# Routed expert layer on one core: when second choices are dispatched, which drain closes a stage, and where the second group's gate stands

## The reference, cut to what matters

```
logits = xf @ gate_w + gate_b
top_vals, top_idx = top_k(softmax(logits), 2)            # 16 experts, 2 chosen
a = silu(xf @ w1[e] + b1[e]) * (xf @ w3[e] + b3[e])      # inner width 176
y = sum over the two choices of  top_val * (a @ w2[e] + b2[e])
z = silu(xf @ sw1 + sb1) * (xf @ sw3 + sb3) @ sw2 + sb2  # shared expert, width 352
x = x + 0.5 * (y + z)
```

## Time and profile before

| what | value |
|---|---|
| median of 3 runs | 1052.64 us (1049.37, 1052.64, 1054.99) |
| the profiled execution's own time | 1053.46 us |
| its span in the trace | 1051.7 us |
| granted TensorE clock, mean | 0.891 |
| busy: TensorE / VectorE / ScalarE / POOL | 803.1 / 588.3 / 468.7 / 590.6 us |
| `front` first pass, `experts`, `attention` | about 0 to 238, to 443.8, to 589.5 us |
| `front` second pass, `experts`, `combine` | to 811.0, to 1017.5, to 1051.7 us |
| sends of `front` (L316) | 256, 252.8 us busy |

### The profile page before, as it was taken

The page is one execution under the profiler, slowest core; times in us unless marked ns, Lnnn a source line. Parts: engine busy times, 40 slices in busy tenths (PEclk is TensorE's granted clock), DMA queues, the critical chain, the costliest instruction groups (busy, mean ns, idle before and its releaser), DMA issues. The chain is left out here.

```text
span 1051.7 us, 20394 instructions
## 1 busy us (share of the span) xinstructions
PE 803.1 (76%) x5408; PEld 718.9 (68%) x5409; DVE 588.3 (56%) x1989; ACT 468.7 (45%) x926; POOL 590.6 (56%) x600
## 2 busy tenths in 40 slices
PE   2899999607999999328989489999810999999910
PEld 2677787507999999326777468877710999999910
DVE  6577766404555555256885477776600555555526
ACT  3466564104555555134664256575200555555500
POOL 2446777753777777532220146677774477776730
PEclk9999999858999999757999679998965999999965
DMA  9812221312333333232200001111231333333339
GB/s 276 118 38 60 66 63 51 95 43 77 101 103 101 103 104 96 68 133 81 80 0 1 0 22 34 40 49 49 61 88 39 89 101 101 103 101 103 94 132 374
DMA packets 82819, 90.42 MB, mean 86 GB/s; under 512 B 20414, under 2 KB 69451, under 8 KB 80715
## 3 DMA queue, kind: packets, MB, share of 16 engines
q1 hardware_dynamic: 63052, 45.42, 16.9%
q0 software_dynamic: 17408, 35.95, 10.2%
q10 hardware_dynamic: 2304, 8.39, 2.0%
HBM read 47.46 MB, written 44.37 MB: 87 GB/s over the span
## 5 line engine op out<-in xcount | busy, mean ns | idle before, releaser
L873 POOL DMA_INDIRECT ys<-e_y,e_x x288 | 275.8, 958 | 139.8 <-issue 87.8
L316 POOL DMA_INDIRECT xs<-f_xrow,f_slot x256 | 252.8, 987 | 87.6 <-issue 75.3
L992 PE MATMUL e_py<-w,e_at 97*128 (+1 forms) x1152 | 152.2, 274 | 0.0
L992 PEld LDWEIGHTS e_py<-w,e_at 97*128 97x128 f32 (+1 forms) x1152 | 139.9, 191 | 0.2 <-issue 0.2
L917 ACT ACTIVATE e_xth<-e_px 128x256 fp32r<-128x256 f32 x144 | 55.2, 384 | 171.4 <-PE e_px L956 171.4
L897 DVE TENSOR_TENSOR e_a<-e_pu,e_sil 128x352 f32<-128x352 f32 x144 | 75.5, 525 | 96.9 <-ACT e_sil L923 91.6
L956 PE MATMUL e_px<-ident,e_x 128*128 128x128 f32 x288 | 57.7, 282 | 90.7 <-DMA e_x<-xs 86.4
L904 DVE TENSOR_SCALAR e_y<-e_py,e_x 128x128 f32<-128x128 f32 x288 | 87.8, 346 | 58.0 <-PE e_py L992 57.9
L756 PEld LDWEIGHTS f_pz<-sw,f_gated 128*128 128x128 f32 (+1 forms) x768 | 102.6, 195 | 9.3
L649 ACT ACTIVATE f_sil<-f_phg,sb 128x512 f32<-128x512 f32 (+1 forms) x96 | 64.7, 685 | 97.9 <-PE f_phg L742 97.6
L468 DVE SCALAR_TENSOR_TENSOR f_gated<-f_phg,sb,f_sil 128x512 f32<-128x512 f32 (+1 forms) x96 | 71.7, 747 | 63.8 <-ACT f_sil L649 54.4
(11 more groups left out here) (160 smaller groups left out, 1431.7 us busy)
## 6 DMA issues: line engine op xcount, KB each, us to landing
e_x<-xs SPq DMA_DIRECT2D x288, 65.0 KB
t_yt<-ys SPq DMA_DIRECT2D x8, 1024.0 KB, 4.9
c_yt<-ys SPq DMA_DIRECT2D x8, 1024.0 KB, 10.4
ys<-e_y,e_x POOLq DMA_INDIRECT x288
xa<-in_attn_x ACTq DMA_DIRECT2D x8, 512.0 KB, 10.3
xs<-f_xrow,f_slot POOLq DMA_INDIRECT x256, 2.4
out<-xa ACTq DMA_DIRECT2D x8, 512.0 KB
f_raw<-in_ffn_w SPq DMA_DIRECT2D x32, 88.0 KB
```

What stands on the lines that cost most here:

```text
L316: pool.indirect_dma_start(xs, bass.IndirectOffsetOnAxis(slot[:, q, i:i + 1], 0), xrow[:, i, :], None).then_inc(done, 16)
L873: pool.indirect_dma_start(ys, bass.IndirectOffsetOnAxis(xin[r][:, t, D:D + 1].bitcast(I32), 0), y[r][:, t, :], None).then_inc(sent[r], 16)
L992: last = pe.matmul(p_y[r][:, t * D:(t + 1) * D], at[r][0:rows_, q], w2, start=c == 0, stop=c == 1, skip_group_check=True)
```

## The change

Three things are changed.

1. POOL's loop sends the second choices of group g - 1, no longer of g - 2, behind the first choices of group g, and ends one turn earlier. To that end `rewrite(s - 2)` on VectorE moves from the end of step s to a place ahead of hot(s) in the same step.
2. In step 1 alone, hot(1), sums(1) and places(1) on VectorE stand directly behind indices(1), and count(1) on TensorE stands ahead of the first `ups`.
3. All four kinds of Blocks are opened with `no_gpsimd_drain=True`: at the Block's end the other engines execute a plain DRAIN and then all five meet at a barrier of semaphores alone, without POOL's DRAIN. `phase` is not touched.

```diff
-        with nc.Block() as block:
+        with nc.Block(no_gpsimd_drain=True) as block:
...
-                for g in range(GROUPS + 2):
+                for g in range(GROUPS + 1):
...
-                    if g >= 2:
-                        pool.wait_ge(rewrote, g - 1)
+                    if g >= 1:
+                        pool.wait_ge(rewrote, g)
                         pool.sem_inc(passed, 1)
-                        send(g - 2, 1, sent1)
+                        send(g - 1, 1, sent1)
...
                     if gating:
                         largest(s)
                         indices(s)
+                    if s == 1:
+                        hot(s)
+                        sums(s)
+                        places(s)
                     gates(m)
...
                     gates(m + 2)
-                    if gating:
+                    if s >= 2:
+                        rewrite(s - 2)
+                    if gating and s != 1:
                         hot(s)
...
-                    if gating:
+                    if gating and s != 1:
                         sums(s)
...
-                    if gating:
+                    if gating and s != 1:
                         places(s)
...
-                    if s >= 2:
-                        rewrite(s - 2)
...
                         if i == 0 and gating:
                             gating_mm(s)
+                        if i == 0 and s == 1:
+                            count(s)
                         ups(m)
...
                         if i == 3 and gating:
-                            count(s)
+                            if s != 1:
+                                count(s)
```

## The result

| | before | after |
|---|---|---|
| median of the runs | 1053.82 us (4 runs, 1049.37 to 1055.17) | 1027.74 us (4 runs, 1026.74 to 1029.63) |
| the profiled execution's own time | 1053.46 us | 1027.63 us |
| its span | 1051.7 us | 1025.9 us |
| mean granted TensorE clock | 0.891 | 0.892 |

The ratio is 0.9762 (95% interval 0.9728 to 0.9796): 26 us faster. The forecast was 1045.8 us, and the result lies outside its range; the first rival, "the drains vanish", had 1029.3 us.

The account below looks back on a forecast made before the run. POOL's sends without a pause were taken to bound front. 1053.46 - 16.6 (part 1) + 9.8 (part 2) + 0 (part 3) = 1046.7 us, or 1045.8 us against the runs' median; range 1040 to 1051.5 us.

Parts of the forecast that it names:

- the drains vanish: Rival: the four long POOL DRAINs at the ends of front and experts go away; 16.5 us gained, 1029.3 us, chance 0.13.
- this end of the sum: Part 3's upper end at the Block ends: 16.5 us gained if the DRAIN's length hangs on the first barrier alone.
- cover of some 0.6 us: At stage ends, clearing semaphores ahead of the L72 DRAIN could cover this much per stage if it is partly plain waiting.
- both theories: At stage ends: the L72 DRAIN pays in full (0 us gained), or the long DRAINs vanish (16.5 us gained).
- The SBUF rule: GpSimd cannot write descriptors during VectorE two-port operations: 620 ns alone, 3100 overlapped; 40 us more if all 16 moved sends met one.
- the 1.9 us for the clock: Part 2, step 1 on TensorE: the pause delays the clock's rise, costing 0.4 + 1.5 us in the two passes.
- the 7.9 us of plain delay: Part 2, step 1: first `ups` wait 4.6 us longer per pass; less savings, 4.2 and 3.7 us.
- the 651 us expected for the second run: Second pass: POOL's run of sends without a pause was to begin at the `scales` of group 4, about 651 us.
- The change to the order brings nothing: Rival: step 1's pause or VectorE's mid-step waits cancel part 1; within 3 us of 1052.6, say 1051 us, chance 0.08.
- The clock stays low: Rival: TensorE's granted clock stays at 0.5 through step 1; part 2 costs 27.3 us, total 1063 us, chance 0.05.

Follow-up runs that it names:

- e5: The changed kernel with a plain POOL DRAIN added at the end of front and experts, in the second pass behind four tiles of zeros; 1044.4 us (one run).
- e6: The changed kernel with a full barrier put into `phase` ahead of the clearing of semaphores; 1042.93 us, ratio 0.9925 to the kernel before.
- e7: The changed kernel with plain POOL DRAINs ahead of the last 8 sends, behind the landing (two in a row in the second pass) and at experts' start; 1034.34 us.
- e1: The kernel before with only the Blocks' end changed (`no_gpsimd_drain=True` at all four Blocks); 1035.49 us, ratio 0.9857.
- e3: The changed kernel without the early gate, step 1 as before (parts 1 and 3); 1020.84 us, ratio 0.9704 to the kernel before.
- e4: The changed kernel without the early dispatch, second choices two groups behind as before (parts 2 and 3); 1042.80 us, ratio 0.9919 to the kernel before.
- e2: The changed kernel with the old Block end at all four Blocks (parts 1 and 2); 1043.39 us, ratio 0.9923 to the kernel before.
- e8: The kernel e3 with second choices of groups 0 and 1 sent without lag and their rewrites moved along; 1019.21 us, ratio 0.9709 to the kernel before.
- e9: The kernel e8 with second choices of group g - 1 ahead of `scales(g + 3)` and later rewrites at their step's end; 1009.91 us, ratio 0.9597.

## Why the prediction was wrong, and where it was right

**Part 3 failed, and it is 16.0 of the 18.1 us by which the forecast missed.** The step is the sentence "I take it that the L72 DRAIN becomes that one and pays in full: 0 us". Right was that a DRAIN is long where it is the first plain one behind sends (e5, e6, e7) and that the long ones lay on the path (e1: 16.4 us against 16.5 for this end of the sum). Wrong was that the one at L72 would be the first. Between the Block's end and L72 stands the reset DRAIN of L71 and the clearing; I had noted them only as cover of some 0.6 us. In the trace of before they always came behind the Block's own DRAIN, so nothing in it told what they do behind sends. e6 shows it: ahead of them the plain DRAIN takes 3.99 us, behind them 0.05. The reason that I gave for taking 0 ("every short DRAIN in the trace has a clean POOL ahead of it") held for both theories: behind L71 POOL is clean as well, by whatever made it so. With both ends of the term equally unseen, 0.13 for the rival was too little.

**Part 1 was right in its mechanism, place and size.** The idle time of POOL between groups 2 and 3 is gone, the run starts with the `scales` of group 4, and it lasts 148.4 us, where the sum had 148.3. By medians the part gives 14.7 to 15.1 us, of 16.6. The rewrite in mid-step shows no cost: the one wait for first choices is 7.2 us, as before 7.0. The second pass is as forecast: from the `scales` of group 4 to the last send it is 7.2 us shorter (e1: 632.99 to 789.71, e3: 628.33 to 777.88), of 7.5. The missing 1.5 to 2 us are in the first pass. There the last send comes 7.1 us sooner (e1: 227.00, e3: 219.87), of 9.1, because the stretch from the `scales` of group 4 to it, though 9.9 us shorter, starts 2.7 us later (68.69, 71.41); from e4 to the changed kernel it starts 2.8 us later too (71.86, 74.68). The rise of the clock in step 1 is later in both pairs (40.75 to 44.08 us, 43.48 to 47.54). Part 1 changes nothing in step 1 on VectorE or TensorE, and the kernel before has these `scales` at 72.10 us without it, so whether part 1 causes this delay isn't shown.

**The SBUF rule.** I had left the penalty for a send beside VectorE's two-port operations in the range. The longest of the 256 sends is 1.56 us now (source view of L316) and was 1.64 us, though 16 more of them run beside VectorE:

```profile
L316 POOL DMA_INDIRECT xs<-f_xrow,f_slot x256: 954/958/1562, 30.0 to 784.5; - x128
```

The longest in any run here took 2.24 us (e2). By that, the 3100 ns that the Trainium skill (SBUF — State Buffer, "SBUF: two separate sides" and the section behind it) gives for an overlapped send was met by none of them in this kernel. No row names the mode of a VectorE operation, so whether any send met a two-port one isn't shown.

**Part 2 was right in sign and place, too large in size.** No gain, as argued: POOL waited 12.74 us ahead of `scales(3)` and 9.30 ahead of `scales(4)` in the changed kernel, slot(1) being there long before. The first `ups` came 4.40 us behind the gate's sum (4.4 forecast). The cost is 6.9 to 7.3 us, of 9.8, and the `scales` of group 4 stand 3.3 and 3.9 us later than in e3, 7.2 together. The over-sized term is mainly the 1.9 us for the clock, above all the 1.5 us of the second pass; the 7.9 us of plain delay were too large by the remaining 0.6 to 1.0. I had assumed the rise to the higher level (2.4 GHz) 6 us behind the first `ups`; it came 3.5 us behind. The term was also too large by its own rows: a matmul of 0.63 us in place of 0.39 loses 0.38 of a slow stretch, not nearly half, which makes 1.4 us of the 1.9. And the 651 us expected for the second run left out what the first pass gains; with it the same sum gives about 646.

**What was luck.** e2, parts 1 and 2 with the old Block end, is 8.5 us under the kernel before, where I had 6.8. That is nearer than its terms: both were too large, by 1.7 and 2.7 us, and the errors offset each other.

**The rivals.** "The drains vanish" was right in what happens to the rows and, at 1029.3 us, within 2 us of the result. The reason given with it, a length that "hangs on something that only the first barrier has", is wrong: e5 and e6 have the full length away from that barrier. And its time holds the same offsetting errors. "The change to the order brings nothing" falls with e2 (8.5 us). "The clock stays low" falls with the rows of step 1: the matmul of 512 columns takes 0.39 us again at 607.27 us.

**Where the time went.** 26.1 us = 16.0 for four DRAINs, 14.9 for the early dispatch, less 7.1 for the early gate, and 2.3 us left over. Of these 2.0 are the difference between two sets of runs of the kernel before (1053.82 and 1051.87 us), and 0.3 are within the noise.

## What to carry to other kernels

Where a cost hangs on the first instruction behind something, look at each instruction between the old place and the new one before taking it that the cost only moves; one that never stood in that position in the trace can be the one that clears it, and then it deserves a chance near one half. When one engine issues without a pause to the end of a stage, sum from the last wait before that run, and after each move look for the next wait behind it (e8 gained nothing until e9 took the following one away). Work brought forward is worth nothing when another wait stands ahead of its consumer, and it may cost the engine that is made to wait for it.

## What was not expected of the hardware

- POOL's plain DRAIN costs 0.082 to 0.088 us for each indirect DMA sent since the last one, even when all have landed: 9.22 us behind 112 sends, 0.71 us behind 8. Other work of 1.9 us ahead of it takes nothing off.
- Behind 120 sends it is still 10.38 us, behind 128 and 144 only 3.99 and 3.65 us, less than behind 80. Why isn't known.
- The reset DRAIN with the clearing of semaphores (L71) takes 0.17 + 0.44 us behind 128 sends, the same as behind a DRAIN of 4.6 us, and the plain DRAIN behind it takes 0.05 us.
- The same 128 sends leave a DRAIN of 4.64 us in one order and 3.99 in another.
